# New slot tables for the steady turns and the last back part of a four-stage sequence kernel

## What is computed

```python
# stage 0: a grid step
df = -(grad(A[0]*f, rows) + grad(A[1]*f, cols)) + 0.5*(grad2(B[0]*f, rows) + grad2(B[1]*f, cols) + mixed(B[2]*f))
x = relu(f + df * dt)
# stage 1: adapter, layer norm over a row
h = gelu(x @ down_W.T + down_b)                        # 256 -> 64
h = h @ expert_W[id].T + expert_b[id] + domain_emb[id]
x = layernorm(h @ up_W.T + up_b + x) * ln_gamma + ln_beta
# stage 2: normalised over the whole 256 x 256 tile, scale and shift from a time embedding
o = silu(scale * tile_norm(x) + shift) @ W_in + b_in
o = silu(scale * tile_norm(o) + shift) @ W_out + b_out
x = o + x
# stage 3: attention block, 16 heads of 16, bias fside, key mask
y = layernorm(x) * (1 + ada_scale) + ada_shift
q, k, v = y @ Wq + bq, y @ Wk + bk, y @ Wv + bv
p = softmax(where(mask, -inf, q @ k.T / 4 + fside))    # per head
x = x + (p @ v) @ Wo + bo
h = layernorm(x) * g2 + beta2
z = h @ W1 + b1                                        # 256 -> 1024
out = x + (z * sigmoid(1.702 * z)) @ W2 + b2
```

## Time and profile before

| | |
|---|---|
| median of three runs | 919.7 us (919.68, 919.7, 922.29) |
| the profiled execution | 922.17 us, its span 920.4 us |
| busy: PE, DVE, ACT, POOL | 858.6, 742.2, 729.5, 237.2 us |
| mean granted TensorE clock | 0.985 of full speed |
| one steady turn | 104.60 us |
| in it busy: PE, ACT, DVE | 101.01, 90.80, 90.68 us |

### The profile page before, as it was taken

One profiled execution on the slowest core, in us unless ns is written; L12 is line 12 of the kernel. 1 busy time (PEld: TensorE's weight loads), 2 busy tenths in 40 slices (PEclk: granted clock), 3 DMA queues, 4 the chain that ended last, 5 costly groups with the idle time before them and its releaser, 6 DMA issues.

```text
span 920.4 us, 18271 instructions
## 1 busy us (share of the span) xinstructions
PE 858.6 (93%) x5712; PEld 665.7 (72%) x5797; DVE 742.2 (81%) x2372; ACT 729.5 (79%) x1904; POOL 237.2 (26%) x237
## 2 busy tenths in 40 slices
PE   8776978999999999999999999999999999999988
PEld 8564657777777777777777777777777777777767
DVE  8757798888898888888898898898898898876542
ACT  2234879989798879979798888979798888978773
POOL 2232223332222323232132323223123323121000
PEclk9986999999999999999999999999999999999999
DMA  9826463734445463744446462754446363655500
GB/s 253 244 67 183 130 191 100 206 118 118 139 144 158 136 164 95 204 123 138 138 127 173 119 166 90 192 151 135 126 147 175 99 167 108 166 156 143 164 17 24
DMA packets 133098, 130.90 MB, mean 142 GB/s; under 512 B 18281, under 2 KB 123497, under 8 KB 132985
## 3 DMA queue, kind: packets, MB, share of 16 engines
q1 hardware_dynamic: 101616, 112.02, 42.7%
q10 hardware_dynamic: 31386, 17.71, 7.0%
HBM read 112.61 MB, written 17.07 MB: 141 GB/s over the span
## 4 chain that ended last, share of the span: by engine, by line
PE 58%; ACT 19%; DVE 8%; issue 3%; POOL 0%; ACTq 0%; DVEq 0%
PE ff_ps L1427 11%; PE ff_ps L1408 9%; PE PT_ps L1463 8%; ACT Pr L1120 5%; PE G L1191 5%; PE scores_ps L1448 4%; PE G L1183 4%; PE ctx_ps L1485 3%; DVE bias L956 3%; ACT L1120 3%; PE scores_ps L1445 2%; PE ff_ps L1394 2%; ACT ffT L1101 2%; ACT tanh L1097 2%; ACT PT L1133 2%
## 5 line engine op out<-in xcount | busy, mean ns | idle before, releaser
L1120 ACT ACTIVATE Pr<-bias,nmax 128x256 f32<-128x256 f32 x512 | 255.8, 506 | 35.5 <-DVE nmax L956 34.8
L956 DVE CUSTOM_DVE_ANT_0 bias<-scores_ps,bias 128x256 f32<-128x256 f32 x512 | 194.1, 420 | 47.1 <-PE scores_ps L1448 26.7
L1133 ACT ACTIVATE PT<-PT_ps 128x512 f32<-128x512 f32 x256 | 152.4, 596 | 50.8 <-PE PT_ps L1463 46.1
L1463 PE MATMUL PT_ps<-ident,Pr 128*128 128x128 f32 x1024 | 156.0, 274 | 8.1 <-ACT Pr L1120 8.1
L574 POOL TENSOR_TENSOR rstd<-var,half_neg 128x2 f32<-128x2 f32 (+1 forms) x64 | 43.4, 678 | 389.8 <-DVE var L709 244.5
L1463 PEld LDWEIGHTS PT_ps<-ident,Pr 128*128 128x128 f32 x1024 | 119.9, 141 | 16.9 <-ACT Pr L1120 13.3
L1408 PE MATMUL ff_ps<-ctxT,w 128*128 128x256 f32 x480 | 117.2, 387 | 13.0 <-ACT ffT L1101 10.7
L1427 PE MATMUL ff_ps<-w,ffT 128*128 128x256 f32 x480 | 112.9, 381 | 0.0
L1408 PEld LDWEIGHTS ff_ps<-ctxT,w 128*128 128x128 f32 x480 | 86.3, 190 | 33.0 <-ACT ffT L1101 16.2
L1448 PE MATMUL scores_ps<-k_stack,q_stack 96*128 96x256 bf16 x512 | 99.2, 275 | 6.0 <-issue 2.0
L1120 ACT ACTIVATION_READ_ACCUMULATOR Pr<-bias,nmax 128x1 f32 x512 | 100.6, 196 | 0.0
(11 more groups left out here) (232 smaller groups left out, 1615.8 us busy)
## 6 DMA issues: line engine op xcount, KB each, us to landing
bias<-in_fside_Bx16xSxS_dram SPq DMA_DIRECT2D x256, 256.0 KB, 3.2
part_dram<-front ACTq DMA_DIRECT2D x32, 384.0 KB, 2.8
q_stack<-part_dram SPq DMA_DIRECT2D x32, 192.0 KB, 3.8
k_stack<-part_dram SPq DMA_DIRECT2D x32, 192.0 KB, 3.7
F<-in_x_dram SPq DMA_DIRECT2D x16, 256.0 KB, 3.7
ada<-rows_dram SPq DMA_DIRECT2D x16, 256.0 KB, 4.7
q_stack<-part_dram SPq DMA_DIRECT2D x32, 128.0 KB, 3.8
k_stack<-part_dram SPq DMA_DIRECT2D x32, 128.0 KB, 3.5
```

What stands on the lines that cost most here:

```text
L956: nc.vector.tensor_tensor_reduce(out=t, in0=SP_[:, n % 2, q * S:(q + 1) * S], in1=t, scale=-1.0, scalar=BIG, op0=ALU.add, op1=ALU.min, acc ...
L1120: ins = nc.scalar.activation(Pr[:, n % PR, q, :], bias[:, n // CH % RING, 2 * (n % CH) + q, :], ACT.Exp, bias=nmax[:, n, q:q + 1], scale=-1.0,
L1133: nc.scalar.activation(PT[:, m % BATCH, :, :].rearrange("p c q -> p (c q)"), TP[:, m % 2, :], ACT.Identity).then_inc(pt_ok, 1)
L1463: ins = pe.transpose(TP[:, m % 2, c * S + q * P:c * S + (q + 1) * P], Pr[:, m % PR, q, c * P:(c + 1) * P], ident[:, :])
```

## The change

Nearly every number of `AT` and every one of `AT_LAST` is new. In `AT_FIRST` one number changes, `xn3` of sequence 0 from 20.5 to 19, which moves no instruction against another. The rest of that table is the old one in other line breaks. No instruction is added or taken away, and the lines below the tables stand two further down (L1408 becomes L1410). Cut to three rows of the tables:

```diff
...
-      "hT": (23, 40.5), "x5b": (30.25, 47.5), "w1": ((25, 26.25, 28, 29.75), (41.75, 42.75, 43, 45.75)),
...
-      "k_out": (28, 41.75), "v": (28.75, 46), "V": (29, 46.5), "mask": (20, 2)}
...
+      "hT": (23.25, 40.75), "x5b": (40.5, 43.75), "w1": ((25.25, 26.75, 28.25, 29.25), (41.5, 43.25, 43.5, 45.5)),
...
+      "k_out": (26.75, 41.75), "v": (29, 43.25), "V": (30, 48.25), "mask": (20, 2)}
...
```

More of the change, by code:

```diff
@@ L72 @@
            "masks": 0}
-AT = {"x4": (27.75, 46.25), "ctx_spread": (19.5, 40.5), "ctx": (19.75, 36.25), "ctx_scale": (19.5, 36.25),
[4 rows of a table removed]
-      "out": (35, 51.25), "store": (36.75, 57.5), "prods_p": (0.5, 18.75), "prods": (0.75, 14), "diffs": (2, 16.5),
[8 rows of a table removed]
-      "q_split": (25.5, 40.25), "q_out": (25.25, 42), "k": (25.5, 41), "kf": (25, 40.5), "k_split": (26.75, 41.75),
-      "k_out": (28, 41.75), "v": (28.75, 46), "V": (29, 46.5), "mask": (20, 2)}
[L89 to L95, removed]
[7 rows of a table removed]
@@ L103 @@
-AT_LAST = {"ctx_spread": (23.25, 34.5), "ctx": (20.5, 30.75), "ctx_scale": (20.5, 30.75), "wo": (22, 33.75),
[4 rows of a table removed]
-           "w2": ((31.25, 37, 47, 48.25), (67, 73.25, 75.75, 77.5)), "out": (55.25, 70), "store": (57, 68.75)}
+AT = {"x4": (32.5, 41.75), "ctx_spread": (17.5, 39.25), "ctx": (20.25, 36.75), "ctx_scale": (20, 36.5),
[5 rows of a table added]
+      "store": (48.75, 54.75), "prods_p": (1, 15), "prods": (1.75, 12.75), "diffs": (2.75, 16),
+      "edges": (2.75, 16.25), "l0": (4.25, 18.75), "x1": (5.5, 18.5), "relu": (5.25, 18.75), "x1_turn": (6.25, 20),
+      "x1T": (7, 19.5), "res1": (12, 23.5), "down": (8.25, 20.75), "hid": (8.25, 20.5), "expert": (9.25, 22),
[8 rows of a table added]
@@ new lines @@
+AT_FIRST = {"s_gelu": (3.25, 3.25), "s_sin": (0.25, 0.25), "s_se": (2.75, 2.75), "s_trig": (3.5, 3.5),
+            "s_onehot": (4, 4), "s_grid": (4.25, 4.25), "s_h1": (3, 3), "s_h2": (3.5, 3.5), "s_h2t": (3.75, 3.75),
+            "s_sel": (2, 2), "s_cond": (4.5, 4.5), "s_condt": (6.25, 6.25), "s_mask": (24.25, 24.25),
+            "s_rows": (15.25, 15.25), "x4": (28, 46.75), "s_fill": (4.25, 4.25), "s_bq": (7.75, 7.75),
+            "s_w2": (34.25, 34.25), "prods_p": (0.25, 5.5), "prods": (5.5, 6), "diffs": (5.5, 6.5),
[8 rows of a table added]
+            "q_out": (28, 40.75), "k": (22.5, 40.75), "kf": (28, 40.5), "k_split": (22.25, 41), "k_out": (29, 42.75),
+            "v": (28.5, 43.25), "V": (25.75, 44)}
@@ L109 @@
+AT_LAST = {"ctx_spread": (24.25, 34.75), "ctx": (21, 30.75), "ctx_scale": (22.25, 30.75), "wo": (23.5, 33.75),
[4 rows of a table added]
+           "w2": ((54.5, 57.25, 58.5, 60), (76.75, 80.5, 85.5, 86.5)), "out": (73.5, 83.25), "store": (76, 77.75)}
 SP_AT = {"front": (0, 7), "stacks": (1, 2, 9, 11), "mask": 6, "rows": (12, 3)}
```

## The result

The changed kernel takes 913.06 us (median of 9 runs, 910.43 to 916.41) against 919.72 us before (9 runs): a ratio of 0.9921, 95% interval 0.9900 to 0.9941. The forecast was 911.5, a ratio of 0.991. The profiled execution took 916.15 us, its span is 914.3.

What follows compares the result with a forecast made beforehand. PE was taken as the bound, busy 101.01 of 104.60 us a turn. The terms, -10.5 + 10.2 - 5.6 - 1.1 - 1.2 = -8.2 us, took the 919.7 median to 911.5, range 905 to 923.

Steps and rivals of the forecast that it cites:

- Part 1: Quarters w1.1/1 and w1.1/2: longer covers remove both waits for ACT's second pass, 1.5 us a turn, 10.5 over seven turns.
- Part 2: w_in.0 without v.1 ahead of it: a new wait for y0, 1.7 us a turn, 10.2 over six turns.
- The bare chain: At w_in.0: y0 ready 5.73 us after w1.1/2, PE there after 4.92, so a 0.81 us wait.
- the term for DVE's delay: Statistics ahead of head 11's maximum delay its exponentials by 1.23 us; 0.51 to 1.23 goes through to w_in.0.
- the filling of 0.1: At w_in.0: 0.1 us of filling after PE's standstill, added to the new wait.
- Part 3: Second half of the turn: waits for exponentials and an evacuation shrink, 0.8 us a turn, 5.6 over seven turns.
- Part 4: Turn 0: stat0 comes earlier, so PE's 3.16 us wait at avg0 shortens by 1.1 us.
- the case priced at -2.8: Turn 0 behind avg0: the shorter standstill leaves the clock at 2.4 GHz, returning 1.7 us more.
- Part 5: Last turn's tail: less work ahead of the last exponentials, more behind them; -1.2 us in sum, bounds -2.0 and +0.9.
- the slower one: Rival: y0.0 comes one head late, w_in.0 waits 3.64 us in six turns, total 923.1 us; chance 0.15.
- No change: Rival: waits move and stay, w_in.0 loss at its upper bound, second half gains nothing, 919.5 us; chance 0.21.
- Every wait goes: Rival: all PE waits, 2.8 us a turn, vanish, total 897.8 us; chance 0.06.

Runs made afterwards that it cites:

- v.1 alone back: Changed kernel with only v.1 put back ahead of w_in.0, head 11 staying ahead of w1.1/1: 915.57 us, ratio 0.9941.
- The run without the quarters: Changed kernel with w1.1/1 again ahead of head 11, w1.1/2 behind it and v.1 ahead of w_in.0: 914.19 us, ratio 0.9925.
- a step and a block of seven: Kernel before with w2.0/0 ahead of head 31: 931.69 us, 1.0121; kernel before with the block around heads 19 and 20 as changed: 951.48 us, 1.0347.

## Why the prediction was right, and where a term was not

The time, 913.06, lies 1.6 us above the forecast and well inside the range; the forecast gain of 8.2 us stands against 6.7 in the medians and 8.8 from the first head on in the profiles. By its terms:

- **Part 1 (1.5 us a turn) was right.** Undoing it brought back 0.60 and 0.78 us, and with v.1 alone back the third quarter waited 1.66. What was placed between a group and the one that needs its bank decided each of these waits. Between starts it is 1.82 less 0.19, or 1.63: the cover of 0.86 was just short of the 0.95 that the third quarter lost.
- **Part 2 (1.7) was too dear; it measured 1.25.** The bare chain was right: 0.81 forecast, 0.77 between starts where the statistics are not moved. Of the term for DVE's delay, 0.51 to 1.23, only 0.14 came through at `w_in`, and nothing of it in the period. The step that failed was to let the delay of the maximum count in full as a delay of ACT, but for the idle of 0.72 behind the exponentials. The maximum had been ready 0.36 us before ACT came to it, so that the kernel before already allowed no more than 0.15. On the other side the filling of 0.1 was undersized: 0.34 were lost behind `w_in`, because `times_v` and w2 wait for ACT and DVE themselves.
- **Part 3 (0.8) was right in size, not in its working.** The run without the quarters puts it at 0.94. The waits for Pr went as forecast, and 1.8 us went in all; but "nothing put in their place" did not hold, 0.9 is new. Nor did single moves with longer covers do it: a step and a block of seven cost 1.4 and 4.6 us a turn when moved alone. In both, work of DVE came late that the changed kernel has in another order; that the new order on DVE is what made the difference fits these rows, but no run moved only the two together.
- **Part 4 (-1.1) failed.** The wait at `avg0` fell by 0.99, but w_in came 1.54 later behind it, and turn 0 became 0.5 us longer. The sentence that failed is "DMA queues and POOL's steps keep a cover of whole heads; I cost them at nothing": in turn 0 two tables meet, and a step of `AT_FIRST` that did not move got in the way of one of `AT` that did. It cost 1.0 us at this place, 1.4 of the whole. The clock, which the term left out, stayed at 1.00 behind `avg0`, the case priced at -2.8, but that time went into the wait at `w_in`, and behind it the clock fell.
- **Part 5 (-1.2) was right:** -1.17 added to the kernel before, +1.16 taken from the changed one.

In turn 3 1.33 us was gained where the terms gave 0.6; five whole steady turns (from `l0.0` of pair 2 to that of pair 7, 523.46 and 516.33 us) bring 7.1, more than five times 1.33 because two of the five took 104.8 and 104.9 us before. Turn 0 costs 0.5 instead of bringing 1.1, and the last stretch brings 2.2. That is 8.8. Two errors of opposite sign, part 2 and part 4, partly paid for each other, so that the nearness of the total to the forecast is partly luck; the sign and the places of the steady turn's gain and loss are not.

Of the rivals, the slower one (a wait of over 3.5 us at `w_in`) did not come: 0.74 us. "No change" had ACT keeping the waits: refuted by the waits that vanished with ACT's busy time unchanged (90.80 and 90.81). "Every wait goes" did not come either: 1.5 us of labelled waits are left in a turn, and groups of eight matmuls that wait for nothing stand 1.73 us apart as before (424.94 to 426.67). Nothing in these runs came near the 26 us of room that the share of weight loads suggested.

## What to carry to other kernels

Where one engine is nearly full, cost a new order by covers: between a step and the one that needs its result, add up what stands in the full engine's queue, and compare it with the chain on the other engines. Count it from start to start: labels of waits are too short, and short waits have none. The sum was good to about a tenth of a us for waits that the order made or removed. It failed where the slack of a step in the middle was left out (the maximum that was ready before ACT came to it), and where a step's other customers were: before moving a step, list everything that it covers on every queue (here `w_in` also covered `times_v`), and look at the seams where two tables meet. And a gain of a whole table may not be divisible: a step and a block of steps moved alone, with the other engines' queues left as they were, made this kernel 1.2 and 3.5% slower.
